# Polynomial layer of a four-layer graph network: TensorE's program for the ten terms written out instead of a hardware loop

## The reference

```python
deg = segment_sum(ones, row); dinv = where(deg > 0, 1 / sqrt(deg), 0)
norm = dinv[row] * dinv[col]
def L_apply(h):
    return h - segment_sum(norm[:, None] * h[col], row)
out = 0; h_k = x; inv_f = 1.0
for k in range(11):                   # K = 10
    out = out + h_k @ W[k] * inv_f
    if k < 10:
        h_k = -L_apply(h_k)
        inv_f = inv_f / (k + 1)
x = layernorm(x + out + bias)
```

## Time and profile before

| | us |
|---|---|
| median of 3 runs (lowest, highest) | 1738.2 (1737.69, 1739.01) |
| the profiled execution | 1737.73 |
| its span, first to last instruction | 1735.7 |
| PE busy in it | 1461.2 (84%) |
| DVE busy | 1141.1 (66%) |
| ACT busy | 481.9 (28%) |
| matmuls of line 1705 (terms) | 6250, 246 ns each |
| products of line 1691 | 250 records |
| last matmul of the terms ends | at 1706.1 |

### The profile page before, as it was taken

The page is one execution under the profiler, slowest core; times in us unless marked ns, Lnnn a source line. Parts: engine busy times, 40 slices in busy tenths (PEclk is TensorE's granted clock), DMA queues, the critical chain, the costliest instruction groups (busy, mean ns, idle before and its releaser), DMA issues. The chain is left out here.

```text
span 1735.7 us, 43832 instructions
## 1 busy us (share of the span) xinstructions
PE 1461.2 (84%) x16295; PEld 1351.0 (78%) x16295; DVE 1141.1 (66%) x3435; ACT 481.9 (28%) x910; POOL 44.6 (3%) x64
## 2 busy tenths in 40 slices
PE   0845428996997999999999969689999999999993
PEld 0534316776997788888888858679999999999993
DVE  5999837884436455555555547667767677676775
ACT  0269718993102343443434321000000000000000
POOL 1100000000000000000000012000000000000000
PEclk9978759997999999999999989889999999999996
DMA  1000014442001644445232233000000000000000
GB/s 20 7 0 0 0 28 139 133 144 75 2 2 39 167 116 133 130 115 149 70 104 69 69 83 82 6 1 2 2 3 2 3 2 2 3 2 3 2 2 21
DMA packets 36999, 83.92 MB, mean 48 GB/s; under 512 B 22926, under 2 KB 23942, under 8 KB 36848
## 3 DMA queue, kind: packets, MB, share of 16 engines
q1 hardware_dynamic: 32216, 74.42, 15.1%
q10 hardware_dynamic: 4410, 7.43, 1.7%
q0 software_dynamic: 224, 0.13, 0.0%
HBM read 60.76 MB, written 21.14 MB: 47 GB/s over the span
## 5 line engine op out<-in xcount | busy, mean ns | idle before, releaser
L1705 PE MATMUL L_psA<-L_parts,mat 125*128 125x192 bf16 x6250 | 517.2, 246 | 0.0
L1705 PEld LDWEIGHTS L_psA<-L_parts,mat 125*128 125x128 bf16 x6250 | 515.5, 98 | 1.1 <-DVE L_parts L1783 1.0
L1174 PEld LDWEIGHTS L_ps_pre<-L_drow,mat 128*128 128x128 bf16 x2250 | 128.5, 98 | 30.3 <-issue 1.1
L1340 DVE TENSOR_TENSOR L_e<-L_ps_z,L_eb 128x512 f32<-128x512 f32 x76 | 52.5, 691 | 132.7 <-PE L_ps_z L1184 132.5
L1770 DVE TENSOR_REDUCE L_sumr<-L_psA 125x64 f32<-125x192 f32 x250 | 89.4, 358 | 76.4 <-PE L_psA L1705 74.2
L1174 PE MATMUL L_ps_pre<-L_drow,mat 128*128 128x32 bf16 (+3 forms) x2250 | 132.8, 212 | 0.0
L659 DVE TENSOR_TENSOR onehot<-iota_bf,codes 128x1024 bf16<-128x1024 bf16 x150 | 98.7, 686 | 29.8 <-PE ps_extra L722 23.0
L771 PE MATMUL L_psA<-L_gparts,mat 125*128 125x192 bf16 x1250 | 112.6, 253 | 4.5 <-DVE L_gparts L784 4.5
L1647 ACT COPY L_wk<-L_Wk 128x64 f32 (+1 forms) x10 | 2.0, 242 | 404.5 <-PE L_psA L1705 404.5
L771 PEld LDWEIGHTS L_psA<-L_gparts,mat 125*128 125x128 bf16 x1250 | 108.8, 102 | 5.5 <-DVE L_gparts L784 4.8
L1168 PE MATMUL L_ps_pre<-mat,L_pp 125*128 125x512 bf16 x375 | 102.9, 383 | 2.5 <-DVE L_pp L1306 2.5
(11 more groups left out here) (296 smaller groups left out, 2365.4 us busy)
## 6 DMA issues: line engine op xcount, KB each, us to landing
L_drow<-rows_d SPq DMA_DIRECT2D x25, 728.0 KB
m_d<-panel SPq DMA_DIRECT2D x25, 684.2 KB
mat<-rows_d SPq DMA_DIRECT2D x25, 640.0 KB, 4.3
mat<-m_d SPq DMA_DIRECT2D x16, 684.2 KB
mat<-m_d ACTq DMA_DIRECT2D x9, 684.2 KB
L_drow<-rows_d SPq DMA_DIRECT2D x25, 84.5 KB
m_d<-panel SPq DMA_DIRECT2D x25, 79.4 KB
mat<-m_d SPq DMA_DIRECT2D x16, 79.4 KB
```

Source lines behind the costliest of these rows:

```text
L1174: last = nc.tensor.matmul(ps_pre[bank][:, to:to + n], w, drow[k][:, of:of + n], start=False, stop=(r == 2 and cc == pieces[-1][0]))
L1340: nc.vector.tensor_tensor(grp(e2_of(k, g)), grp(ps_z2[bank]), eb2[:].unsqueeze(1).broadcast_to([P, len(tiles), H]), ALU.add).then_inc(bias ...
L1705: last = nc.tensor.matmul(ps[:, 0:3 * D], t.mat[0:B, kb, b * B:b * B + P], parts[src][:, kb].rearrange("p r d -> p (r d)"), start=(kb == 0 ...
```

## The change

In PE's program the hardware loop over pairs of terms becomes a loop of the Python that writes the program. The five iterations stand one behind the other, and the semaphore values are constants. The loops of DVE and ACT stay as they are, and so does every matmul and its order.

```diff
-                with pe.Fori(0, KMAX, 2) as it:
-                    it = it.with_bounds(min_val=0, max_val=KMAX - 2)
+                for it in range(0, KMAX, 2):
                     products(it)
                     term(it, 0)
-                    term((it + 1).with_bounds(min_val=1, max_val=KMAX - 1), 1)
+                    term(it + 1, 1)
```

## The result

| | before | changed |
|---|---|---|
| median (executions beside each other) | 1737.95 us (4) | 1724.4 us (4) |
| lowest, highest | 1737.31, 1739.01 | 1719.57, 1726.39 |
| ratio, 95% interval | | 0.9917 [0.9896, 0.9938] |
| the profiled execution | 1737.73 us | 1719.57 us |
| its span | 1735.7 us | 1715.5 us |

Predicted were 1723.3 us in a range of 1721.6 to 1728.8.

A forecast was written before the change was run, and what follows sets the result against it. PE was taken to set the layer's end. Gaps -9.45, clock -4.82, seam -0.5 and head -0.2 gave -14.9 us, from 1737.73 to 1722.8; with the median's 0.47, 1723.3 us, range 1721.6 to 1728.8.

The forecast's parts named there:

- The gap is the jump: PE's four "issue" gaps between one iteration's last matmul and the next's first product are the jump back; they go, -9.45 us.
- The clock: Three of four product groups after gaps ran at reduced clock; without a gap no fall was expected, -4.82 us.
- The seam: Step from a term's bf16 matmuls to the next float32 products: 5.6 us per boundary against 5.72, -0.5 us in all.
- The head: Before PE's first product an unconditional jump and two register set-ups go, the wait on DVE stays: -0.2 us.
- Priced at nothing: Block 0's register additions and run-time waits are hidden by moving columns; fetching the longer PE program costs nothing.
- DVE next: DVE's copies of product 24 come about 5.0 us after the block's end, covered by products with 0.4 to 0.6 us spare.
- Clock falls anyway: Rival: float32 products draw the clock down without a gap; 1728.1 us with three falls, 1729.8 with four; chance 0.10.
- Part of the gap stays: Rival: PE's gap holds more than a jump, such as draining its queue; half left gives 1728.0 us; chance 0.05.
- The jump was never the gap: Rival: switching from queued bf16 matmuls to float32 costs 2.4 us four times; only 0.2 us go, 1738.0; chance 0.04.
- The straight program starves: Rival: PE's fivefold longer program waits for instruction fetches; at 2.4 us a piece, 1843 us; chance 0.03.
- The sum against the median: -14.9 us takes the profiled 1737.73 to 1722.8; the runs' median lies 0.47 higher, so 1723.3 us.

The follow-up runs named there:

- the kernel with two jumps: Against the kernel before, PE's first and last pair of terms written out, the three between kept in a loop; median 1730.07 us, ratio 0.9954.
- changed kernel with early products: Changed kernel with the first group of products begun before DVE has split the last parts, products 8 to 15 last; median 1719.71 us, ratio 0.9891.

## Why the prediction was right, step by step

- *The gap is the jump.* Right. The gap vanished with the jump (-9.45 us in the sum), moved with it to bf16 matmuls, and went from four to two when the jumps did. The comparison with DVE's own gap of 2.8 us was the argument that carried. The Trainium skill's figures for branches (Advanced Engine Details and Errata, Control Flow Timing: about 51 and 108 ns) are far from the 2.0 to 2.6 us per jump back measured here; they may fit the forward entry, where no gap shows, but not a long loop's end. The measurement decides. What PE does in these 2 us is not shown. The prediction took them as agreeing with a stall for a fetch, but no instruction piece moved on any queue in the four gaps of the kernel before: a piece of 16 KB came 0.4 to 0.6 us before the last matmul's end, the next ones within 1.1 us behind the restart.
- *The clock.* Right in kind, and now shown for its cause. No later group fell in three profiles of the changed kernel (12 groups), and all four fell behind a gap of 1.95 us that had no jump. The size was 4.82 us for three falls; the second profile of the kernel before has four. One reading was off: the first of these groups ran at half clock until 1261.8 us, not 1261.4 (0.59 in the earlier trace rows for that us), and nothing hung on it.
- *The seam.* Taken at 5.6 us, measured 5.49; the bounds were 5.45 and 5.9. Four boundaries: 37.14 to 21.95, -15.2 us, where the sum had -14.7. The row with 111 ns per float32 matmul was slightly too high: 5.24 us for 48 are 109.
- *The head.* Taken at -0.2, measured 0.31 to 0.04, -0.27. Another 0.2 came from the first group of products, 7.95 to 7.74 us. That is chance: it took 8.45 and 7.87 in the other two profiles of the changed kernel.
- *Priced at nothing.* Fetching: right. The queue that serves PE shows the same pieces in a stretch of terms of the changed kernel as in the earlier trace rows:

```profile
q8 instruction: 10, 0.16, 0.7%
```

  The register additions: right for this change, since they leave with the loop, but the reason given was incomplete. "The moving columns cover them" holds only while the wait ahead of the block is met early. In the kernel before it was: the gap and the slow products put the products' end 3.2 to 4.8 us behind the copies. A version that closes the gap and keeps the additions loses 0.7 to 1.0 us in a first block, as the entry of the kernel with two jumps did.
- *DVE next.* The cover was put at 0.4 to 0.6 us and measured 0.43 (copies 5.06 us after the block's end, products 5.49). Taking DVE's jump away moved nothing inside the layer but 0.09 us a pair, so the cover held.
- *The rivals.* Clock falls anyway: no. Part of the gap stays: no. The jump was never the gap: no. The straight program starves: no, the terms stayed at 103.28 us.
- *The sum against the median.* 1723.3 predicted, 1724.4 measured in the first four, 1723.16 and 1723.97 after. The layer won 15.7 us, 0.8 more than the sum, 0.5 of it in the seam. The working took the profiled execution's 2.0 us outside the span as given. That is one of two levels, and all 15 executions of the changed kernel were on the upper one. This was not foreseen, and it was small: 15.7 us less half a microsecond is the 15.2 of the means. The two misses have opposite signs, so that the total came within 0.3 us of the sum is in part luck; each term alone lay within its bounds or 0.01 us beside them.

What stays open: what PE does in the 2 us of a jump, and why the time outside the span sits at one level for one program and at two for another. Ten thousand further instructions went with 0.9 us more of it, and writing out DVE's loop with 1.4 to 1.7 us less; nothing else was tried for it.

## What to carry to other kernels

A hardware loop on the engine that sets the end costs time at each jump back: here 2.0 to 2.6 us of standing still, and then up to 1.9 us more because TensorE's clock fell behind most of these pauses. Look for "issue" at a loop's end on the critical engine, price the slow work behind it as well, and write the loop out only on that engine; DVE's jump of 2.8 us beside it cost nothing inside the layer. What drew the clock down was the pause and not the jump: a wait of 1.95 us put into the straight program undid the whole gain, and one of 0.54 us cost only itself and 0.24 us.

## What the runs showed of the hardware that was not expected

- Gaps of PE of 0.54 us: no fall of the clock in 4. Gaps of 1.95 us without a jump: a fall in 4 of 4. Gaps of 2.0 to 2.5 us at jumps before float32 products: in 14 cases in four profiles and three programs 12 falls, and the two groups that kept the clock stood behind the longest gap of their profiles (2.49 and 2.42 us), so the length alone does not decide. Behind jumps between bf16 matmuls (2.1 to 2.6 us): 1 of 3 in one kernel, 3 of 3 in the other, at about 0.9 us a fall.
- Register additions between PE's matmuls, with the waits that use them, are free or cost 0.7 to 1.0 us per 25 matmuls, depending on when the wait ahead of them is met.
- The entry into a loop and its exit showed no gap; only the jump back did.
- The time outside the span was near 2 or near 4 us: near 4 in all 15 executions of the changed kernel, near 2 in all 19 with DVE's loop written out, mixed in the kernel before (26 of 74 under 3 us) and in the changed kernel with early products (2 of 6).
